# Read lines' norms on GpSimd beside the scans, and one addition for keys and values in the preparation

## The chip, the cores and the metric

The program runs on one core of one Trainium2 chip. The metric is the device time of one execution in microseconds (us), as the median of three runs. The engines are TensorE (PE, with its weight loads as PEld), VectorE (DVE), ScalarE (ACT), GpSimd (POOL) and SyncE (SP); they run side by side and wait for each other by semaphores.

## The reference, cut to what matters

Four layers work on x of 2 x 1024 tokens by 128: an attention (16 heads of 64), a mixture of experts, a second attention (16 heads of 8) whose keys and values are gated, and the experts again. The change lies in what comes ahead of the second attention:

```python
def exterior(p1, p2):                       # 6 products of pairs, per token and head
    L = p1[..., _PI] * p2[..., _PJ] - p1[..., _PJ] * p2[..., _PI]
    n = jnp.clip(jnp.linalg.norm(L, axis=-1, keepdims=True), 1e-12)
    return L / n
write_lines, read_lines = exterior(w1, w2), exterior(r1, r2)
incidence = jnp.einsum('bthp,bshp->bhts', read_lines, write_lines @ J6)
mem_score = jnp.einsum('bhts,hts->bht', incidence ** 2, weights)   # weights: decay ** (t - s), s < t
gram_gate = jax.nn.sigmoid(mem_score * mem_scale[None, :, None])[..., None]
k_enh = k + kv_gate * gram_gate * k_geo
v_enh = v + kv_gate * gram_gate * v_geo
```

## The kernel before

The stages follow each other, each a `Phase` with a block per engine and a barrier at its end. Two of them are touched.

**`geometry` (L1370 to L1757)** makes the gates. Tokens lie on the 128 partitions, eight tiles to each of two batches. ACT copies the projected factors out of PSUM (`moved`, L1523), DVE makes the six components of write and read lines (`cross`, L1633) into `L`. Squared incidence is a sum over 21 products of components. `write_products(b)` (L1649 to L1656) first makes the norms of the write lines from squares that ACT made (`square_write`, L1538), then 21 products; `read_products(b)` (L1672) makes the 15 mixed products of the read lines, while their six squares come from ACT (`square_read`, L1546 and L1547) and stand in the same tile `prod[1]`. The last of the seven instructions of `read_products` waits for them (`read_ready`) and raises `made`, so that PE may transpose. The read lines are not divided by their norm there: `read_scale(b)` (L1638 to L1643, L1681) sums the six squares to `inv`, clips, inverts and multiplies by `mem_scale`, and `weigh(b)` (L1704) applies that to the scores at the end.

PE transposes the products into six PSUM banks (L1491), DVE scans over the tokens (`scan`, L1690) and multiplies (L1698), six scans in all, PE sums (L1460) and turns the scores (L1469), ACT moves them and takes the exponential (L1559, L1553), DVE makes the gates (L1712 to L1714). ACT meanwhile takes sixteen banks of queries in two parts (`queries`, L1530 and L1532), with `square_write(1)` ahead of bank 9 and `square_read(1)` ahead of bank 11; behind the last bank it loads the table of the exponential and makes `dec_e` from the decay (L1584), for which DVE waits before it makes `row_decay` (L1744, L1745) and starts the scans. GpSimd adds the two parts of the queries (L1416), sixteen additions of 128x512, and starts on them when DVE has cleared the first column of the scans (`zeroed`, L1747).

The order on DVE is written out by hand:

```python
            cross(1, slice(0, 2))
            read_scale(0)
            write_products(1)
            read_products(1)
            read_scale(1)
            dve.wait_ge(dec_exp, 1)
```

then the scans of batch 0, two of batch 1, `weigh(0)`, the last scan, `gates(0)`, `weigh(1)`, `gates(1)`.

**`prepare_b` (L1760 to L1847)** makes keys and values of sixteen tiles, in rings of three buffers. PE projects a tile to 512 columns (L1800); DVE multiplies the geometric half by the gate (L1834, `geo`); GpSimd adds the bias (L1847) and, ahead of that, clears the rest of the values' rows (L1844); DVE adds the keys (L1823, `key`) and the values (L1824, into `V9`); ACT makes the rounded copies of the keys (L1812, `rep`); DVE makes their rest (`low`, L1829); PE transposes (L1791) and ACT moves the result to `KS4` (L1815). In its turn i DVE does `geo` of tile i, the additions of tile i-1 and `low` of tile i-2; PE does the projection of tile i and the transposes of tile i-3.

Of the kernel before, what the change touches and what calls it, by code (L numbers as in the profile page):

```python
# [13 lines left out]
P = 128  # L14
# [1352 lines left out]
def geometry(nc, X, stats, xn, xnT, w_geo, sel, decay_logits, scale_row, kv_gate, gate, ident, constants, w_q, q_bias, q_scale, QS4):  # L1367
# [4 lines left out]
    with Phase(nc, "geo") as ph:  # L1372
# [18 lines left out]
        read_ready = ph.sem("read_ready")  # L1391
        turned, used = ph.sem("turned"), ph.sem("used")
        scored, s_moved, flipped = ph.sem("scored"), ph.sem("s_moved"), ph.sem("flipped")
# [14 lines left out]
        @block.gpsimd  # L1408
        def _(pool):
            constants()  # L1410
            pool.wait_ge(zeroed, len(M))
            for k in range(QK):
                g, t = k // 4, k % 4
                dst = QS4[:, g, t * BANK:(t + 1) * BANK]
                pool.wait_ge(q_ready, 2 * k + 2)
                nc.gpsimd.tensor_tensor(dst, dst.bitcast(F32), q_rest[:, g, t * BANK:(t + 1) * BANK], ALU.add)  # L1416
# [174 lines left out]
        def _(dve):  # L1591
# [42 lines left out]

            def norms(b, w, sq):

                n2, part = inv[:, b, w, :, :], T2[:, w * QT:(w + 1) * QT, 0:3, :]
                link(nc.vector.tensor_tensor(part.rearrange("p n c h -> p n (c h)"), sq[:, :, 0:3, :].rearrange("p n c h -> p n (c h)"),  # L1638
                                             sq[:, :, 3:6, :].rearrange("p n c h -> p n (c h)"), ALU.add))
                link(nc.vector.tensor_tensor(n2, part[:, :, 0, :], part[:, :, 1, :], ALU.add))  # L1640
                link(nc.vector.tensor_tensor(n2, n2, part[:, :, 2, :], ALU.add))
                link(nc.vector.tensor_scalar(n2, n2, 1e-24, None, ALU.max))
                link(nc.vector.reciprocal(n2, n2))  # L1643

            def write_products(b):

                line, scaled, out = L[:, b, 0:QT, :, :], T2[:, 0:QT, :, :], prod[0][:, b * QT:(b + 1) * QT, :, :]
                dve.wait_ge(squared, b + 1)
                norms(b, 0, T1[:, 0:QT, :, :])  # L1649
                link(nc.vector.tensor_tensor(scaled, line, inv[:, b, 0, :, :].unsqueeze(2).to_broadcast([P, QT, 6, H]), ALU.mult))  # L1650
# [25 lines left out]

            def read_scale(b):

                dve.wait_ge(lines, 2 * BATCH)
                norms(b, 1, prod[1][:, b * QT:(b + 1) * QT, 0:6, :])  # L1680
                link(nc.vector.tensor_tensor(inv[:, b, 1, :, :], inv[:, b, 1, :, :], scale_row[:, :].unsqueeze(1).to_broadcast([P, QT, H]),  # L1681
                                             ALU.mult))

            def scan(b, g):
# [11 lines left out]
                for c in range(2):  # L1696
                    dve.wait_ge(turned, n + c + 3)
                    nc.vector.scalar_tensor_tensor(RM[j % 3][:, c * BANK:(c + 1) * BANK], bank[(n + 2 + c) % NB][0:ROWS, :],  # L1698
                                                   row_decay[0:ROWS, 0:1], m[:, c * BANK:(c + 1) * BANK], ALU.mult, ALU.mult).then_inc(used, 1)

            def weigh(b):
# [36 lines left out]
            cross(1, slice(0, 2))  # L1738
            read_scale(0)
            write_products(1)  # L1740
            read_products(1)
            read_scale(1)
            dve.wait_ge(dec_exp, 1)
# [7 lines left out]
            scan(1, 0)  # L1751
            scan(1, 1)
            weigh(0)
            scan(1, 2)
            gates(0)
            weigh(1)
# [3 lines left out]
def prepare_b(nc, xnT, w_kv, kv_bias, gate, KS4, V9, ident):  # L1760
# [4 lines left out]
    with Phase(nc, "prep_b") as ph:  # L1765
        geo = [ph.sb(f"geo{i}", [P, 2, H, B_DH]) for i in range(NB)]
        key = [ph.sb(f"key{i}", [P, H, B_DH]) for i in range(NB)]
        rep = [ph.sb(f"rep{i}", [P, NG, GRP, REP, B_DH]) for i in range(NB)]
        kv_ps = [ph.psum(f"kvp{i}", [P, 4, H, B_DH]) for i in range(NB)]
        k_ps = [ph.psum(f"kp{i}", [P, BANK]) for i in range(NB)]  # L1770
        kv_done, gated, biased = ph.sem("kv_done"), ph.sem("gated"), ph.sem("biased")
        keyed, kv_read = ph.sem("keyed"), ph.sem("kv_read")
        high_done, rep_done = ph.sem("high_done"), ph.sem("rep_done")
# [6 lines left out]
        def key_copies(i):  # L1780
            return key[i % NB][:, :, :].unsqueeze(2).to_broadcast([P, H, REP // 2, B_DH])

        @block.tensor
        def _(pe):
# [10 lines left out]
            for i in range(TILES + 3):  # L1795
                if i < TILES:
                    at, b = 1 + (i % QT) * P, i // QT
                    if i >= NB:
                        pe.wait_ge(kv_read, i - NB + 1)
                    nc.tensor.matmul(kv_ps[i % NB][:, :, :, :].rearrange("p w h d -> p (w h d)"), xnT[:, b, at:at + P], w_kv[:, :],  # L1800
# [5 lines left out]
        def _(act):  # L1806
            for i in range(TILES + 2):
                if i < TILES:
                    act.wait_ge(keyed, i + 1)
                    if i >= NB:  # L1810
                        act.wait_ge(k_done, i - NB + 1)
                    nc.scalar.activation(copies(i, 0).bitcast(F32R), key_copies(i), ACT.Copy).then_inc(high_done, 1)  # L1812
                if i >= 2:
                    act.wait_ge(k_done, i - 1)
# [4 lines left out]
        def _(dve):  # L1819
            def add_geo(i):  # L1820

                dve.wait_ge(biased, i + 1)
                nc.vector.tensor_tensor(key[i % NB][:, :, :], kv_ps[i % NB][:, 0, :, :], geo[i % NB][:, 0, :, :], ALU.add).then_inc(keyed, 1)  # L1823
                nc.vector.tensor_tensor(V9[:, i, :, 0:B_DH], kv_ps[i % NB][:, 1, :, :], geo[i % NB][:, 1, :, :], ALU.add).then_inc(kv_read, 1)  # L1824

# [282 lines left out]
```

## Time and profile before

| | |
|---|---|
| median of 3 runs | 1117.47 us (1116.43 to 1118.13) |
| the profiled execution, its own time | 1119.37 us |
| its span, first to last instruction | 1117.6 us, granted TensorE clock 0.924 of full |
| busy | PE 968.8 us (87%), DVE 763.7 (68%), ACT 593.1 (53%), POOL 336.3 (30%) |
| `geometry` | 627.4 to 705.2 us of the span |
| `prepare_b` | 705.5 to 734.6 us |
| second attention | from 734.9 us |

Busy time is a sum over stages that are bound by different engines; what an edit is worth is read in its own stage, from the start times of neighbouring instructions on one engine and from what each waits for. Times in the rows further down are microseconds from the start of the span.

### The profile page before, as it was taken

The numbers are of one execution on the slowest core, as the hardware profiler recorded it, in microseconds if no ns is written. First come the engines' busy times: TensorE is split into PE (matmuls) and PEld (weight loads), VectorE is DVE, ScalarE is ACT, GpSimd is POOL, SyncE is SP. The second block draws the span as 40 slices with busy tenths as digits, with TensorE's granted clock in tenths as the row PEclk, the third lists the DMA queues.
The fourth block names the chain that finished last, engine by engine and source line by source line (L and its number), as shares of the span: only waits on it lengthen the run. The fifth ranks groups of instructions, "written<-read, shape, count | busy, mean of one in ns | idle before, by whom it ended". The sixth has DMA issues, their size and how long they took to land. (4 is left out here: it accounts for less than half of the span.)

```text
span 1117.6 us, 18644 instructions
## 1 busy us (share of the span) xinstructions
PE 968.8 (87%) x6218; PEld 625.2 (56%) x6218; DVE 763.7 (68%) x2256; ACT 593.1 (53%) x1165; POOL 336.3 (30%) x422
## 2 busy tenths in 40 slices
PE   6989999999999999999739376789999999996474
PEld 4767667666667667766429333344444444443363
DVE  6767758775767758777513699787888888863423
ACT  4866657666767658666212291324555555564121
POOL 3522122211221113210144207453644343521523
PEclk9999999999999999999859697868999999999577
DMA  6630000000000000000340100000000000000623
GB/s 206 134 94 2 1 1 1 1 1 1 1 1 1 1 1 1 2 1 1 101 147 29 48 1 0 1 1 1 1 2 1 1 2 1 1 1 13 192 58 99
DMA packets 49402, 32.23 MB, mean 29 GB/s; under 512 B 9195, under 2 KB 45980, under 8 KB 49308
## 3 DMA queue, kind: packets, MB, share of 16 engines
q1 hardware_dynamic: 47260, 26.78, 8.5%
q0 software_dynamic: 2048, 4.26, 1.2%
q8 instruction: 50, 0.82, 0.3%
q14 instruction: 44, 0.36, 0.1%
HBM read 21.44 MB, written 11.69 MB: 30 GB/s over the span
## 5 line engine op out<-in xcount | busy, mean ns | idle before, releaser
L561 ACT ACTIVATE attn_a_prob<-attn_a_score,attn_a_m_all 128x128 f32<-128x128 f32 (+7 forms) x256 | 188.7, 740 | 49.9 <-DVE attn_a_m_all L481 45.8
L911 ACT ACTIVATE attn_b_probT<-attn_b_st 128x1024 f32<-128x1024 f32 (+1 forms) x192 | 145.1, 808 | 131.8 <-PE attn_b_st L777 130.5
L477 DVE TENSOR_REDUCE attn_a_m_far<-attn_a_score 128x1 f32<-128x512 f32 (+3 forms) x192 | 105.6, 550 | 71.5 <-PE attn_a_score L389 68.3
L401 PE MATMUL attn_a_slot<-tab,attn_a_prob 128*128 128x128 f32 x1152 | 149.2, 274 | 0.2
L401 PEld LDWEIGHTS attn_a_slot<-tab,attn_a_prob 128*128 128x128 f32 x1152 | 131.8, 141 | 9.8 <-issue 1.6
L413 PE MATMUL attn_a_o<-attn_a_ptsb,Vd 128*64 128x512 f32 x288 | 136.3, 603 | 0.0
L413 PE MATMUL attn_a_o<-attn_a_ptsa,Vd 128*64 128x512 f32 x288 | 136.3, 603 | 0.0
L840 DVE CUSTOM_DVE_ANT_0 attn_b_slot<-attn_b_slot,later 128x128 f32<-128x128 f32 (+3 forms) x256 | 118.7, 522 | 18.7 <-PE attn_b_slot L752 18.4
L570 ACT ACTIVATE attn_a_ptsa<-attn_a_slot 128x512 f32<-128x512 f32 x144 | 85.7, 595 | 85.9 <-PE attn_a_slot L401 85.4
L752 PE MATMUL attn_b_slot<-KS,attn_b_alone 128*128 128x512 f32 (+2 forms) x384 | 125.6, 424 | 2.7 <-POOL attn_b_alone L933 2.2
L481 DVE CUSTOM_DVE_ANT_0 attn_a_score<-attn_a_score,bias_near,attn_a_m_far 128x256 f32<-128x256 f32 (+2 forms) x192 | 107.4, 559 | 6.8
L490 DVE COPY attn_a_ptsb<-attn_a_slot 128x512 f32<-128x512 f32 x144 | 99.1, 688 | 14.7 <-PE attn_a_slot L401 14.5
L614 POOL COPY attn_a_wide<-attn_a_rinv 128x512 f32<-128x512 f32 x32 | 19.6, 614 | 290.9 <-issue 269.1
L752 PEld LDWEIGHTS attn_b_slot<-KS,attn_b_alone 128*128 128x128 f32 x384 | 63.5, 200 | 73.1 <-DVE attn_b_least L845 20.6
L845 DVE TENSOR_REDUCE attn_b_least<-attn_b_slot 128x1 f32<-128x512 f32 x128 | 80.7, 684 | 19.9 <-PE attn_b_slot L752 19.2
L949 POOL TENSOR_SCALAR_AFFINE_SELECT attn_b_probT<-attn_b_probT 128x256 f32<-128x256 f32 x128 | 51.3, 406 | 124.6 <-ACT attn_b_probT L911 123.3
L792 PE MATMUL attn_b_pv<-attn_b_probT,V 128*32 128x512 f32 (+3 forms) x768 | 83.6, 507 | 0.6 <-POOL attn_b_probT L949 0.6
L933 POOL TENSOR_TENSOR attn_b_alone<-QS,tab 128x512 fp32r<-128x512 f32 x64 | 66.3, 1040 | 42.3 <-PE attn_b_slot L752 39.1
L413 PEld LDWEIGHTS attn_a_o<-attn_a_ptsa,Vd 128*64 128x64 f32 x288 | 34.5, 136 | 60.3 <-issue 50.7
L767 PE MATMUL attn_b_st<-QS,KS 32*128 32x512 f32 (+2 forms) x384 | 56.5, 453 | 2.9 <-ACT attn_b_probT L911 2.2
L389 PE MATMUL attn_a_score<-KH,QS_0a 128*128 128x512 f32 (+2 forms) x96 | 38.1, 397 | 15.7 <-ACT attn_a_prob L561 14.0
L561 ACT ACTIVATION_READ_ACCUMULATOR attn_a_prob<-attn_a_score,attn_a_m_all 128x1 f32 x256 | 51.0, 199 | 0.0
(236 smaller groups left out, 1831.1 us busy)
## 6 DMA issues: line engine op xcount, KB each, us to landing
moe_weights_w<-in_L_ffn_w_dram SPq DMA_DIRECT2D x32, 256.0 KB, 3.4
to_experts<-xn SPq DMA_DIRECT2D x2, 1056.0 KB, 11.8
moe_experts_xe<-to_experts SPq DMA_DIRECT2D x16, 132.0 KB, 2.7
bias_by_query_and_key<-bias_by_distance SPq DMA_DIRECT2D x2, 1024.0 KB
bias_near<-bias_by_query_and_key SPq DMA_DIRECT2D x2, 1024.0 KB, 6.3
from_experts<-xn SPq DMA_DIRECT2D x2, 1024.0 KB, 11.7
moe_experts_back<-from_experts SPq DMA_DIRECT2D x8, 256.0 KB, 3.7
X<-in_L_attn_a_x_dram SPq DMA_DIRECT2D x2, 512.0 KB, 4.7
```

The source lines that it names most:

```text
L401: ins = nc.tensor.transpose(dst[:, jj * P:(jj + 1) * P], probs(g)[:, 2 * jj + half, i * P:(i + 1) * P], ident[:, :])
L413: ins = nc.tensor.matmul(o_ps[OWN[half], :], Vd[:, b * QT + i, OWN[half]], pts[half][k % RING][:, :], start=i == 0, stop=i == steps(g) - 1 ...
L477: nc.vector.tensor_reduce(least, score[t % 2][:, at:at + nk - win], AX.X, ALU.min).then_inc(far_done, 1)
L481: nc.vector.tensor_tensor_reduce(out=near, in0=near, in1=bias_near[:, s * HS + j, BANK - win:], scale=1.0, scalar=least, op0=ALU.add, op1= ...
L490: nc.vector.tensor_copy(pts[1][k % RING][:, :], bank[u % SLOTS_S][:, :]).then_inc(moved_b, 1)
L561: nc.scalar.activation(probs(g)[:, j, 0:nk], score[t % 2][:, at:at + nk], ACT.Exp, bias=m_all[:, j:j + 1], scale=-1.0, accum_out=rowsum[g ...
L570: nc.scalar.activation(pts[0][k % RING][:, :], bank[u % SLOTS_S][:, :], ACT.Copy).then_inc(moved_a, 1)
L752: ins = nc.tensor.matmul(s[:, to:to + wide], alone[j % RING][:, a, :], KS4[:, g, at:at + wide], start=True, stop=True)
L792: ins = nc.tensor.matmul(pv[a * 32:a * 32 + VW, lo:], V9[:, b * QT + kt, g * GRP + a, :], probT[n % 2][:, a, lo:], start=kt == 0, stop=end ...
L840: ins = nc.vector.tensor_tensor_reduce(out=s, in0=s, in1=later[:, BANK - w:], scale=1.0, scalar=3e38, op0=ALU.add, op1=ALU.min, accum_out= ...
L845: nc.vector.tensor_reduce(found, s, AX.X, ALU.min).then_inc(slot_free, 1)
L911: nc.scalar.activation(probT[n % 2][:, two, lo:], st[:, two, lo:], ACT.Exp, scale=-1.0).then_inc(exp_done, 1)
```

## The change

In `geometry` the sums of the read lines' squares and their clipping go from DVE to GpSimd, four instructions per batch, after the wait for `zeroed` and ahead of the query additions; the sum of pairs is written over `L`. On DVE `read_scale(b)` keeps the reciprocal and the product with `scale_row`, and stands in the scans: for batch 0 ahead of `weigh(0)`, for batch 1 behind the last scan. `read_products(1)` now comes before `write_products(1)`. In `prepare_b` one DVE addition of 256 columns, keys and values together, goes to a tile `both`; ACT makes the copies from it and moves the values to `V9`.

```diff
@@ geometry, GpSimd
+            def read_scale(b):
+                pool.wait_ge(made, 2 * b + 2)
+                rows = slice(b * QT, (b + 1) * QT)
+                part, n2 = L[:, b, QT:, 0:3, :], inv[:, b, 1, :, :]
+                nc.gpsimd.tensor_tensor(part, prod[1][:, rows, 0:3, :], prod[1][:, rows, 3:6, :], ALU.add).then_inc(summed, 1)
+                pool.wait_ge(summed, 4 * b + 1)
+                nc.gpsimd.tensor_tensor(n2, part[:, :, 0, :], part[:, :, 1, :], ALU.add).then_inc(summed, 1)
+                pool.wait_ge(summed, 4 * b + 2)
+                nc.gpsimd.tensor_tensor(n2, n2, part[:, :, 2, :], ALU.add).then_inc(summed, 1)
+                pool.wait_ge(summed, 4 * b + 3)
+                nc.gpsimd.tensor_scalar(n2, n2, 1e-24, None, ALU.max).then_inc(summed, 1)
+                pool.wait_ge(summed, 4 * b + 4)
             constants()
             pool.wait_ge(zeroed, len(M))
+            read_scale(0)
+            read_scale(1)
             for k in range(QK):
@@ geometry, DVE
             def read_scale(b):
-                dve.wait_ge(lines, 2 * BATCH)
-                norms(b, 1, prod[1][:, b * QT:(b + 1) * QT, 0:6, :])
+                n2 = inv[:, b, 1, :, :]
+                dve.wait_ge(summed, 4 * b + 4)
+                link(nc.vector.reciprocal(n2, n2))
                 link(nc.vector.tensor_tensor(n2, n2, scale_row[:, :].unsqueeze(1).to_broadcast([P, QT, H]), ALU.mult))
...
             cross(1, slice(0, 2))
-            read_scale(0)
+            dve.wait_ge(lines, 2 * BATCH)
+            read_products(1)
             write_products(1)
-            read_products(1)
-            read_scale(1)
             dve.wait_ge(dec_exp, 1)
...
             scan(1, 1)
+            read_scale(0)
             weigh(0)
             scan(1, 2)
+            read_scale(1)
             gates(0)
@@ prepare_b, PE
                     if i >= NB:
-                        pe.wait_ge(kv_read, i - NB + 1)
+                        pe.wait_ge(summed, i - NB + 1)
@@ prepare_b, ACT
-                    act.wait_ge(keyed, i + 1)
+                    act.wait_ge(summed, i + 1)
                     if i >= NB:
                         act.wait_ge(k_done, i - NB + 1)
                     nc.scalar.activation(copies(i, 0).bitcast(F32R), key_copies(i), ACT.Copy).then_inc(high_done, 1)
+                    nc.scalar.activation(V9[:, i, :, 0:B_DH], both[i % NB][:, 1, :, :], ACT.Copy).then_inc(v_moved, 1)
@@ prepare_b, DVE
                 dve.wait_ge(biased, i + 1)
-                nc.vector.tensor_tensor(key[i % NB][:, :, :], kv_ps[i % NB][:, 0, :, :], geo[i % NB][:, 0, :, :], ALU.add).then_inc(keyed, 1)
-                nc.vector.tensor_tensor(V9[:, i, :, 0:B_DH], kv_ps[i % NB][:, 1, :, :], geo[i % NB][:, 1, :, :], ALU.add).then_inc(kv_read, 1)
+                if i >= NB:
+                    dve.wait_ge(v_moved, i - NB + 1)
+                    dve.wait_ge(rep_done, i - NB + 1)
+                nc.vector.tensor_tensor(both[i % NB][:, :, :, :], kv_ps[i % NB][:, 0:2, :, :], geo[i % NB][:, :, :, :], ALU.add).then_inc(summed, 1)
```

Some places of the order follow, with line numbers of the kernel each is from. First GpSimd in `geometry`, from the clearing of `cols` to the query additions (`QS`, `geo_q_rest`). Before:

```order
L2065 MEMSET cols 128x1024 x2
L1416 TENSOR_TENSOR QS<-QS,geo_q_rest 128x512 [waits geo_q_ready,geo_zeroed]
L1416 TENSOR_TENSOR QS<-QS,geo_q_rest 128x512 [waits geo_q_ready] x15
L79 UNCONDITIONAL_BRANCH
L1841 UNCONDITIONAL_BRANCH [waits barrier_Pool_Activation_PE_DVE_SP_gather]
```

and with the change:

```order
L2085 MEMSET cols 128x1024 x2
L1415 TENSOR_TENSOR geo_L<-geo_prod 128x8x48 [waits geo_made,geo_zeroed]
L1417 TENSOR_TENSOR geo_inv<-geo_L 128x128 [waits geo_summed]
L1419 TENSOR_TENSOR geo_inv<-geo_inv,geo_L 128x128 [waits geo_summed]
L1421 ISA
L1421 TENSOR_SCALAR geo_inv<-geo_inv 128x128 [waits geo_summed]
L1415 TENSOR_TENSOR geo_L<-geo_prod 128x8x48 [waits geo_made,geo_summed]
L1417 TENSOR_TENSOR geo_inv<-geo_L 128x128 [waits geo_summed]
L1419 TENSOR_TENSOR geo_inv<-geo_inv,geo_L 128x128 [waits geo_summed]
L1421 TENSOR_SCALAR geo_inv<-geo_inv 128x128 [waits geo_summed]
L1432 TENSOR_TENSOR QS<-QS,geo_q_rest 128x512 [waits geo_q_ready,geo_summed]
L1432 TENSOR_TENSOR QS<-QS,geo_q_rest 128x512 [waits geo_q_ready] x15
```

Eight instructions stand ahead of the first query addition, and with them an `ISA` row that the diff does not name. Before, GpSimd has such a row ahead of the first `AFFINE_SELECT` of the second attention (L949), and with the change it has none there.

Second, DVE from the end of the fifth scan, where `geo_bank` is the transposed products and `geo_z` the weighed scores. Before:

```order
L1704 TENSOR_TENSOR geo_z<-geo_flip,geo_inv 128x128 [waits geo_flipped]
L1690 SCALAR_TENSOR_TENSOR geo_shared<-geo_row_decay,geo_bank 112x512 [waits geo_turned]
L1690 SCALAR_TENSOR_TENSOR geo_shared<-geo_row_decay,geo_shared,geo_bank 112x512 [waits geo_turned,geo_used]
L1698 SCALAR_TENSOR_TENSOR geo_shared<-geo_bank,geo_row_decay,geo_shared 112x512 [waits geo_turned,geo_scored,geo_used]
L1698 SCALAR_TENSOR_TENSOR geo_shared<-geo_bank,geo_row_decay,geo_shared 112x512 [waits geo_turned]
L1712 TENSOR_SCALAR geo_e<-geo_e 128x128 [waits geo_ez]
L1713 RECIPROCAL geo_z<-geo_e 128x128 [waits geo_chain]
L1714 TENSOR_SCALAR gate_b<-geo_z,kv_gate 128x128 [waits geo_chain]
L1704 TENSOR_TENSOR geo_z<-geo_flip,geo_inv 128x128 [waits geo_flipped]
```

and with the change:

```order
L1714 RECIPROCAL geo_inv<-geo_inv 128x128 [waits geo_summed]
L1715 TENSOR_TENSOR geo_inv<-geo_inv,scale_row 128x128 [waits geo_chain]
L1720 TENSOR_TENSOR geo_z<-geo_flip,geo_inv 128x128 [waits geo_flipped,geo_chain]
L1699 SCALAR_TENSOR_TENSOR geo_shared<-geo_row_decay,geo_bank 112x512 [waits geo_turned]
L1699 SCALAR_TENSOR_TENSOR geo_shared<-geo_row_decay,geo_shared,geo_bank 112x512 [waits geo_turned,geo_used]
L1707 SCALAR_TENSOR_TENSOR geo_shared<-geo_bank,geo_row_decay,geo_shared 112x512 [waits geo_turned,geo_scored,geo_used]
L1707 SCALAR_TENSOR_TENSOR geo_shared<-geo_bank,geo_row_decay,geo_shared 112x512 [waits geo_turned]
L1714 RECIPROCAL geo_inv<-geo_inv 128x128 [waits geo_summed]
L1715 TENSOR_TENSOR geo_inv<-geo_inv,scale_row 128x128 [waits geo_chain]
L1728 TENSOR_SCALAR geo_e<-geo_e 128x128 [waits geo_ez,geo_chain]
L1729 RECIPROCAL geo_z<-geo_e 128x128 [waits geo_chain]
L1730 TENSOR_SCALAR gate_b<-geo_z,kv_gate 128x128 [waits geo_chain]
```

The pair of reciprocal and product for batch 0 stands between the fifth and the sixth scan, that for batch 1 behind the sixth.

## Rows read from the trace of the kernel before

**Rows 1.** Busy time by stretch: us, each engine (instructions), TensorE's granted clock, DMA

```profile
713.50:729.10 15.60, 14.69 (x61) 6.88 (x62) 14.69 (x40) 9.02 (x20) 10.82 (x20) 1.00 0.00 1
...
735.00:760.00 25.00, 23.34 (x60) 12.72 (x60) 21.83 (x74) 1.94 (x2) 13.05 (x13) 0.53 0.01 1
```

**Rows 2.** Timeline, DVE, before the scans: start, us, line, operation, count

```profile
660.65 0.56 DVE L1638 TENSOR_TENSOR geo_shared<-geo_prod 128x384 f32<-128x384 f32 x1
...
663.48 0.56 DVE L1638 TENSOR_TENSOR geo_shared<-geo_shared 128x384 f32<-128x384 f32 x1
...
670.18 2.56 DVE L1672 TENSOR_TENSOR geo_prod<-geo_L 128x256 f32<-128x256 f32 x7
672.66 0.55 DVE L1638 TENSOR_TENSOR geo_shared<-geo_prod 128x384 f32<-128x384 f32 x1
...
674.16 0.95 DVE L1643 RECIPROCAL geo_inv<-geo_inv 128x128 f32<-128x128 f32 x1
...
675.48 0.15 DVE L1744 TENSOR_SCALAR geo_dec_e<-geo_dec_e 112x1 f32<-112x1 f32 x1
```

**Rows 3.** Timeline, ACT, the same stretch

```profile
664.46 0.53 ACT L1547 ACTIVATE geo_prod<-geo_L 128x384 f32<-128x384 f32 x1
...
672.99 0.20 ACT L1584 ACTIVATE geo_dec_e<-decay 112x1 f32<-112x1 f32 x1
```

**Rows 4.** Timeline, DVE, the end of the geometry

```profile
695.46 0.28 DVE L1704 TENSOR_TENSOR geo_z<-geo_flip,geo_inv 128x128 f32<-128x128 f32 x1
695.66 1.21 DVE L1690 TENSOR_TENSOR_SCAN geo_shared<-geo_row_decay,geo_bank 112x512 f32<-112x512 f32 x1
...
699.55 0.22 DVE L1712 TENSOR_SCALAR geo_e<-geo_e 128x128 f32<-128x128 f32 x1
...
703.03 0.29 DVE L1704 TENSOR_TENSOR geo_z<-geo_flip,geo_inv 128x128 f32<-128x128 f32 x1 [1.96 <-PE geo_flip L1469]
```

**Rows 5.** Timeline, all engines, one turn of the preparation in full pace

```profile
716.62 0.42 DVE L1834 TENSOR_TENSOR prep_b_geo<-prep_b_kvp,gate_b 128x256 f32<-128x256 f32 x1 [0.18 <-PE prep_b_kvp L1800]
...
716.96 0.28 DVE L1823 TENSOR_TENSOR prep_b_key<-prep_b_kvp,prep_b_geo 128x128 f32<-128x128 f32 x1
...
717.12 0.72 POOL L1847 TENSOR_TENSOR prep_b_geo<-prep_b_geo,kv_bias 128x256 f32<-128x256 f32 x1 [0.61 <-DVE prep_b_geo L1834]
...
717.36 0.78 DVE L1829 TENSOR_TENSOR prep_b_rep<-prep_b_key,prep_b_rep 128x256 f32<-128x256 f32 x1
...
718.19 0.66 PE L1791 MATMUL prep_b_kp<-tab,prep_b_rep 128*128 128x128 f32 x4 [0.18 <-DVE prep_b_rep L1829]
...
718.68 1.02 PE L1800 MATMUL prep_b_kvp<-w_kv,xnT 128*128 128x512 f32 x2
...
719.74 0.42 DVE L1834 TENSOR_TENSOR prep_b_geo<-prep_b_kvp,gate_b 128x256 f32<-128x256 f32 x1 [0.18 <-PE prep_b_kvp L1800]
```

**Rows 6.** Timeline, DVE, the last `low` but one, with GpSimd idle

```profile
732.38 0.41 DVE L1829 TENSOR_TENSOR prep_b_rep<-prep_b_key,prep_b_rep 128x256 f32<-128x256 f32 x1
```

**Rows 7.** Timeline, POOL, the query additions

```profile
676.06 19.67 POOL L1416 TENSOR_TENSOR QS<-QS,geo_q_rest 128x512 fp32r<-128x512 f32 x16 [46.02 <-DVE geo_shared L1747]
```

**Rows 8.** Line L949 on GpSimd and its sequencer: ns min/median/max, first and last start

```profile
L949 POOLq MODIFY_POOL_CONFIG  x2: 11/11/11, 755.0 to 755.1; - x2
```

**Rows 9.** Timeline, POOL, the first instruction of that line

```profile
758.83 0.41 POOL L949 TENSOR_SCALAR_AFFINE_SELECT attn_b_probT<-attn_b_probT 128x256 f32<-128x256 f32 x1 [3.75 <-ACT attn_b_probT L911]
```

**Rows 10.** Line L862 on DVE: ns min/median/max by form

```profile
L862 DVE SCALAR_TENSOR_TENSOR cols<-attn_b_least,cols x8: 190/192/194, 744.4 to 975.1; 128x16 f32<-128x16 f32 x8
L862 DVE SCALAR_TENSOR_TENSOR cols<-attn_b_both,cols x8: 267/352/358, 766.5 to 997.7; 128x16 f32<-128x16 f32 x8
```

**Rows 11.** Timeline, all engines, one of those beside GpSimd

```profile
798.85 0.89 POOL L949 TENSOR_SCALAR_AFFINE_SELECT attn_b_probT<-attn_b_probT 128x256 f32<-128x256 f32 x2 [0.46 <-ACT attn_b_probT L911]
798.95 0.36 DVE L862 SCALAR_TENSOR_TENSOR cols<-attn_b_both,cols 128x16 f32<-128x16 f32 x1
```

**Rows 12.** Timeline, POOL, the second of those two

```profile
799.34 0.41 POOL L949 TENSOR_SCALAR_AFFINE_SELECT attn_b_probT<-attn_b_probT 128x256 f32<-128x256 f32 x1
```

More of the change, by code:

```diff
@@ L1391, in geometry @@
         read_ready = ph.sem("read_ready")
-        turned, used = ph.sem("turned"), ph.sem("used")
+        turned, used, summed = ph.sem("turned"), ph.sem("used"), ph.sem("summed")
         scored, s_moved, flipped = ph.sem("scored"), ph.sem("s_moved"), ph.sem("flipped")
@@ L1633, in cross, with norms @@
                 nc.vector.tensor_tensor(dst, first, second, ALU.subtract).then_inc(lines, halves.stop - halves.start)
-            def norms(b, w, sq):
-                n2, part = inv[:, b, w, :, :], T2[:, w * QT:(w + 1) * QT, 0:3, :]
+            def norms(b, sq):
+                n2, part = inv[:, b, 0, :, :], T2[:, 0:QT, 0:3, :]
                 link(nc.vector.tensor_tensor(part.rearrange("p n c h -> p n (c h)"), sq[:, :, 0:3, :].rearrange("p n c h -> p n (c h)"),
@@ L1648, in write_products @@
                 dve.wait_ge(squared, b + 1)
-                norms(b, 0, T1[:, 0:QT, :, :])
+                norms(b, T1[:, 0:QT, :, :])
                 link(nc.vector.tensor_tensor(scaled, line, inv[:, b, 0, :, :].unsqueeze(2).to_broadcast([P, QT, 6, H]), ALU.mult))
@@ L1675, in read_products @@
                 ins.then_inc(made, 1)
-            def read_scale(b):
-                dve.wait_ge(lines, 2 * BATCH)
-                norms(b, 1, prod[1][:, b * QT:(b + 1) * QT, 0:6, :])
-                link(nc.vector.tensor_tensor(inv[:, b, 1, :, :], inv[:, b, 1, :, :], scale_row[:, :].unsqueeze(1).to_broadcast([P, QT, H]),
-                                             ALU.mult))
             def scan(b, g):
@@ L1699, in scan, with read_scale @@
                                                    row_decay[0:ROWS, 0:1], m[:, c * BANK:(c + 1) * BANK], ALU.mult, ALU.mult).then_inc(used, 1)
+            def read_scale(b):
+                n2 = inv[:, b, 1, :, :]
+                dve.wait_ge(summed, 4 * b + 4)
+                link(nc.vector.reciprocal(n2, n2))
+                link(nc.vector.tensor_tensor(n2, n2, scale_row[:, :].unsqueeze(1).to_broadcast([P, QT, H]), ALU.mult))
             def weigh(b):
@@ L1766, in prepare_b @@
         geo = [ph.sb(f"geo{i}", [P, 2, H, B_DH]) for i in range(NB)]
-        key = [ph.sb(f"key{i}", [P, H, B_DH]) for i in range(NB)]
+        both = [ph.sb(f"both{i}", [P, 2, H, B_DH]) for i in range(NB)]
         rep = [ph.sb(f"rep{i}", [P, NG, GRP, REP, B_DH]) for i in range(NB)]
@@ L1771, in prepare_b @@
         kv_done, gated, biased = ph.sem("kv_done"), ph.sem("gated"), ph.sem("biased")
-        keyed, kv_read = ph.sem("keyed"), ph.sem("kv_read")
+        summed, v_moved = ph.sem("summed"), ph.sem("v_moved")
         high_done, rep_done = ph.sem("high_done"), ph.sem("rep_done")
@@ L1780, in key_copies @@
         def key_copies(i):
-            return key[i % NB][:, :, :].unsqueeze(2).to_broadcast([P, H, REP // 2, B_DH])
+            return both[i % NB][:, 0, :, :].unsqueeze(2).to_broadcast([P, H, REP // 2, B_DH])
         @block.tensor
```

## The prediction

> **What bounds the kernel now.** The chain of waits covers only the end of the span, from 1064.9 us on, and says nothing on the changed stretch; so I read the busy time by stretch first, then the timelines of single engines there. In the preparation's full pace DVE and PE are both busy 14.69 of 15.60 us [rows 1]: a tie, which busy shares can't break. From 660.65 us to the start of the scans DVE goes from instruction to instruction without a wait [rows 2], so it sets the pace there, and through the scans as well; only 1.96 us ahead of the last `weigh` are idle [rows 4].
>
> **Edit 1, in front of the scans: a gain of 2.24 us, not of what leaves DVE.** `read_scale(0)` takes from 660.65 to 663.48, 2.83 us; `read_scale(1)` from 672.66 to 675.48, 2.82 us [rows 2]. So 5.65 us leave this stretch. But the order has changed too. `read_products(1)` lasts 672.66 - 670.18 = 2.48 us, and now starts at 660.65. Its seventh instruction waits for the squares of ACT, which end at 664.46 + 0.53 = 664.99 [rows 3]; before, it came at 672 and waited for nothing. ACT's place for them behind ten banks of queries isn't changed. Without that wait the six first would be through by about 662.9, so DVE stands for 2 us, does the last (0.2) and begins `write_products(1)` at 665.2. That takes 670.18 - 663.48 = 6.70 us [rows 2]: through at 671.9. Then comes the second wait: `dec_e`, the exponential of the decay, which ACT ends at 672.99 + 0.20 = 673.19 [rows 3]. Before, DVE came by at 675.48, long after. Now ACT sets the start of the scans: 673.24 instead of 675.48. **Gain 2.24 us.** ACT's own work there depends on DVE only through `lines`, at 660.6, which doesn't move.
>
> **Edit 2, what comes back inside the scans.** Reciprocal and product are 675.48 - 674.16 = 1.32 us [rows 2]. The pair for batch 0 lies between the fifth and the sixth scan, where DVE has no gap (695.46 to 695.66 is `weigh` alone [rows 4]): it costs its full 1.32 us. The pair for batch 1 lies behind the sixth scan: from there DVE has `gates(0)`, 699.55 to 701.07 by the idle time in the row, then 1.96 us idle until the scores are turned [rows 4]. The pair fills 1.32 of these, 0.64 us are left: nothing. If that cover is gone, each us more costs one.
>
> **Edit 3, two readers of one port.** `low` (L1829) takes 0.78 us in full pace [rows 5] and 0.41 us when GpSimd does nothing [rows 6]. GpSimd's addition beside it runs from 717.12 to 717.84; `low` starts at 717.36 and ends at 718.14, 0.30 us behind that addition, in all turns alike. I read this as `low` standing until GpSimd has read. The same with L862: 0.19 us alone, up to 0.36 beside GpSimd [rows 10]. All of these have two inputs in SBUF; DVE's scans, with one input in PSUM, don't differ beside GpSimd and without it. The product of `inv` and `scale_row` has two inputs in SBUF, and in its new place, about 694.3 us, it meets the query additions, which stand back to back at 19.67 / 16 = 1.23 us each [rows 7]. So it waits between 0 and 1.23 us on the path; nothing in the trace fixes the phase and I take the middle, **0.6 us**. It should get in between two of them: at 798.95 DVE's L862 stood behind the first of two adjacent instructions of GpSimd and ended at 799.31, before the second began at 799.34 [rows 11, 12].
>
> The Trainium skill says the same and draws the line sharply: a DVE instruction with two SBUF inputs and a GpSimd instruction that reads SBUF exclude each other, and the second to issue is blocked for the whole of the first (SBUF — State Buffer, "Who interferes with whom"). By this the trace agrees, with 0.78 against 0.41; the rule speaks against both halves of this change.
>
> **Edit 4, GpSimd's eight instructions.** The addition of 256 columns takes 0.72 us [rows 5], of 512 1.23 us [rows 7]; 384 columns lie between, 1.0, and 128 follow at 0.5. The clipping has one input: not over the 0.41 us of L949's 256 columns [rows 9]. Per batch 1.0 + 0.5 + 0.5 + 0.4 and four semaphores of 0.08 (717.04 to 717.12 [rows 5]) make 2.7 us, 5.4 for both. GpSimd starts 2.24 us earlier, at 673.8, so the query additions begin at 679.2 and end at 698.9. The stage ends at 705.2 (table), now about 704.9: 6 us of cover. The sums are needed at 693.2: no wait.
>
> The `ISA` row is the unknown. Before, it stands in the second attention as MODIFY_POOL_CONFIG at 755.1 [rows 8], and the first instruction behind it starts at 758.83, just when ACT has released it [rows 9]. So such a change of configuration costs between 0 and 758.83 - 755.1 = 3.7 us. Anywhere in that range the query additions end at 698.9 to 702.6, before 704.9, and it costs nothing by itself. Its leaving the second attention gains nothing, as the wait there is for ACT.
>
> The Trainium skill gives about 6 us for the first call after such a load (GPSIMD Engine Reference, "Instruction dispatch"). The trace disagrees for the instruction that it shows, which began 3.7 us behind it. By the page's figure GpSimd would end at 704.9 instead, at the very end of the stage: a result of its own, taken as a rival below.
>
> **Edit 5, the preparation: nothing.** Two additions, together 0.40 us from start to start (716.96 to `low` at 717.36), become one like `geo`, 0.34 us (716.62 to 716.96 [rows 5]): 0.06 us less DVE work per tile, 0.9 us over sixteen. But what follows, `low`, waits for the port until GpSimd's addition is read, and that starts when `geo` ends. The loop is `geo` at 716.62, GpSimd 717.12 to 717.84, `low` to 718.14, transposes from 718.19, projection from 718.68 to 719.70, `geo` at 719.74 [rows 5]: 3.12 us for two tiles, and neither addition is in it. So 0, with 0.9 us as the other end of the range. ACT gets a move of 128 columns more per tile, between its 0.20 us for one column and its 0.53 us for 384 [rows 3], and is busy 9.02 of 15.60 [rows 1], ten tiles: at the most 14.3: covered, and if it weren't, `rep` would come late to `low`. The new waits of DVE, on `v_moved` and `rep_done`, are for three tiles back and are long met; behind them would stand `low`. In the last tile the copies start 0.14 us later, as the joint addition ends later, and ACT ends with at most 0.1 us more.
>
> **The sum**: -2.24 + 1.32 + 0.6 + 0 + 0.05 = -0.3 us. Against the profiled execution's own 1119.37 that is 1119.1; that execution lies 1.90 above the median, so against the median of 1117.47 it is **1117.2 us**. With the ends of each term: -2.24 + 1.32 + 0 - 0.9 = -1.8 to -2.24 + 1.32 + 1.23 + 0.1 = +0.4. 0.2%, or 2.2 us, is about what a measurement can tell from no change here, and all of this lies within it.
>
> **Rivals.**
>
> *The product starves at the port* (slower). GpSimd's query additions queue without a gap. If one takes the port again before DVE gets it, the product stands from 694.3 until they are through, at 698.9 to 702.6 by edit 4: 4.6 to 8.3 us, of which the forecast has 0.6. Time 1121.2 to 1124.9. It decides as soon as DVE loses a second round. For it: sixteen ready additions. Against it: DVE got in at 799.31 [rows 11, 12]. 6%.
>
> *GpSimd gets late* (no change to little slower). With the configuration at 3.7 us or more the query additions are still there when DVE does the product of batch 1 and the steps of `gates(0)`, from 700.2 on; each may wait up to 1.23 us, and only 0.64 us are free ahead of the last `weigh`. Two such waits at 0.6 cost 0.6 us, four full ones over 4. Time 1117.8, at most 1121. GpSimd itself becomes the end only if the eight instructions and the load take over 704.9 - 673.8 - 19.7 = 11.4 us. For it: the price of small additions at strides isn't in the trace. Against: 6 us of cover. 14%, of it 2% beyond 2.2 us.
>
> *The preparation was bound by DVE's total, and the clock moves* (faster). If `low` didn't wait for GpSimd's read, all 0.9 us would come. And PE runs at the lower level, 1.2 GHz, through nearly all of the first 25 us of the second attention (0.53 of full at 735 to 760 [rows 1]), after it stood still at the seam between the stages. DVE's work in there is 21.83 us, so at the full clock it could be up to 25 - 21.83 = 3.2 us shorter. A shift of the start can change which stretches are slow, though nothing in the change shortens the pause. Time 1117.2 - 0.9 - 3.2 = 1113.1. 10%, and 2% for the opposite, a stretch that falls to the lower level.
>
> **How the numbers follow.** The forecast has 68%, 1117.2, its own range 1115.6 to 1118.4 with the scatter of the runs. The late GpSimd (14%) and small gains of the preparation without the clock stay within 0.2% too. Faster by over 0.2%: the clock, 10%. Slower: starvation 6%, a very late GpSimd 2%, the clock 2%, 10% in all. Same: 80%. The range leaves out the clock's gain and the starvation: 1115.0 to 1119.3.
>
> **What would show it.** In the profile after: the seventh instruction of `read_products(1)` starts at about 665.0; `dec_e + 1` starts within 0.1 us of ACT's exponential; the scans start 2.2 us earlier; the first product L1715 lasts 0.3 to 1.5 us, the last scan starts about 0.3 us earlier than before; the query additions end before 703; `low` still lasts about 0.78 and ends 0.3 us behind GpSimd's addition; two tiles still take 3.12 us. I am wrong if the two-tile pace falls to 3.06 or less (then DVE's total counts), if L1715 lasts over 1.6 us (starvation), or if GpSimd starts the query additions later than 685.

## The result: slower by 3.8 us

Over nine runs each, the kernel before took 1118.78 us in the median (1116.43 to 1120.18) and the changed one 1122.63 us (1120.1 to 1123.64). The ratio is 1.0034, with a 95% interval of 1.0025 to 1.0042: 3.8 us slower, 2.8 to 4.7. The forecast was no change, 1117.2, with a range up to 1119.3; the time lies above it. The kernel before itself came out 1.31 us higher over nine runs than over the three that the forecast started from (1118.78 against 1117.47), so the fair comparison is by differences: -0.3 us forecast, +3.8 measured.

### The profile after

Its span is 1120.6 us against 1117.6, at a granted clock of 0.922. Everything in front of the changed code stands about 1.05 us later in this execution (the third `cross` ends at 661.67 against 660.62), which is taken as scatter between executions, since nothing ahead of it was changed, and is taken off wherever stretches are compared.

The timeline of DVE, in front of the scans (columns: start, duration, engine, line, operation, count, and in brackets the idle time before it with what ended it):

```profile
661.70 2.37 DVE L1688 TENSOR_TENSOR geo_prod<-geo_L 128x256 f32<-128x256 f32 x6
666.07 0.29 DVE L1688 TENSOR_TENSOR geo_prod<-geo_L 128x128 f32<-128x128 f32 x1 [2.00 <-ACT geo_prod L1563]
...
674.27 0.15 DVE L1759 TENSOR_SCALAR geo_dec_e<-geo_dec_e 112x1 f32<-112x1 f32 x1 [1.22 <-ACT geo_dec_e L1600]
```

ACT at the same place:

```profile
665.51 0.53 ACT L1563 ACTIVATE geo_prod<-geo_L 128x384 f32<-128x384 f32 x1
...
672.75 1.28 ACT L1600 ACT_TABLE_LOAD   x1
674.04 0.20 ACT L1600 ACTIVATE geo_dec_e<-decay 112x1 f32<-112x1 f32 x1
```

Both waits of edit 1 are there: 2.00 us for ACT's squares, 1.22 us for the exponential of the decay. The scans' first step is at 674.27 instead of 675.48 + 1.05 = 676.53: 2.26 us earlier. That much is gained.

GpSimd, its new instructions and the query additions; then the view of line L1421 with the duration as ns min/median/max; then the same view of the query additions:

```profile
674.86 0.99 POOL L1415 TENSOR_TENSOR geo_L<-geo_prod 128x384 f32<-128x384 f32 x1 [44.13 <-DVE geo_shared L1762]
...
680.41 19.65 POOL L1432 TENSOR_TENSOR QS<-QS,geo_q_rest 128x512 fp32r<-128x512 f32 x16
```

```profile
L1421 POOLq MODIFY_POOL_CONFIG  x2: 7/7/7, 676.9 to 676.9; - x2
L1421 POOL TENSOR_SCALAR geo_inv<-geo_inv x2: 524/532/539, 677.0 to 679.8; 128x128 f32<-128x128 f32 x2
```

```profile
L1432 POOL TENSOR_TENSOR QS<-QS,geo_q_rest x16: 1262/1274/1289, 680.4 to 698.8; 128x512 fp32r<-128x512 f32 x16
```

The eight instructions take 680.41 - 674.86 = 5.55 us, and behind the change of configuration at 676.9 the instruction starts at 677.0: no wait to speak of. The additions end at 700.06. Each lasts 1.27 us, but one starts every 1.23 us: they overlap by 0.04.

DVE and GpSimd around the first product, from the timeline of all engines (a window that begins in it counts only four of the additions), and the end of the stage on DVE:

```profile
694.26 0.94 DVE L1714 RECIPROCAL geo_inv<-geo_inv 128x128 f32<-128x128 f32 x1
...
695.13 4.92 POOL L1432 TENSOR_TENSOR QS<-QS,geo_q_rest 128x512 fp32r<-128x512 f32 x4
695.24 4.96 DVE L1715 TENSOR_TENSOR geo_inv<-geo_inv,scale_row 128x128 f32<-128x128 f32 x1
700.24 0.29 DVE L1720 TENSOR_TENSOR geo_z<-geo_flip,geo_inv 128x128 f32<-128x128 f32 x1
```

```profile
705.31 0.29 DVE L1715 TENSOR_TENSOR geo_inv<-geo_inv,scale_row 128x128 f32<-128x128 f32 x1
...
707.81 0.29 DVE L1720 TENSOR_TENSOR geo_z<-geo_flip,geo_inv 128x128 f32<-128x128 f32 x1 [0.64 <-PE geo_flip L1485]
...
712.40 0.42 DVE L1854 TENSOR_TENSOR prep_b_geo<-prep_b_kvp,gate_b 128x256 f32<-128x256 f32 x1 [2.39 <-PE prep_b_kvp L1817]
```

Here the time went. The product, 0.29 us of work when it stands alone (705.31), lasted 4.96 us, from 0.11 us behind the start of an addition to 0.14 us behind the end of the last one, past four additions. The row shows no idle time: to the profile a stalled instruction is a busy one. The rest is as forecast: the second pair costs nothing, and 0.64 us stay free ahead of the last `weigh`.

One turn of the preparation, DVE, GpSimd and ACT:

```profile
718.27 0.42 DVE L1854 TENSOR_TENSOR prep_b_geo<-prep_b_kvp,gate_b 128x256 f32<-128x256 f32 x1 [0.18 <-PE prep_b_kvp L1817]
...
718.61 0.41 DVE L1844 TENSOR_TENSOR prep_b_both<-prep_b_kvp,prep_b_geo 128x256 f32<-128x256 f32 x1
...
718.77 0.72 POOL L1867 TENSOR_TENSOR prep_b_geo<-prep_b_geo,kv_bias 128x256 f32<-128x256 f32 x1 [0.61 <-DVE prep_b_geo L1854]
718.94 0.84 DVE L1849 TENSOR_TENSOR prep_b_rep<-prep_b_both,prep_b_rep 128x256 f32<-128x256 f32 x1
...
719.38 0.29 ACT L1830 ACTIVATE V<-prep_b_both 128x128 f32<-128x128 f32 x1
...
719.44 0.41 POOL L1864 MEMSET V<- 128x384 f32 x1
...
721.39 0.42 DVE L1854 TENSOR_TENSOR prep_b_geo<-prep_b_kvp,gate_b 128x256 f32<-128x256 f32 x1 [0.18 <-PE prep_b_kvp L1817]
```

721.39 - 718.27 = 3.12 us for two tiles, as in [rows 5]. `low` starts 0.17 us behind the start of GpSimd's addition instead of 0.24, and lasts 0.84 us instead of 0.78; it still ends 0.29 us behind that addition. It got in although GpSimd's next instruction, the `memset` at 719.44, starts 0.05 us before the addition's recorded end; the `memset` has no input, so it reads nothing. Busy time, in the columns of [rows 1], of the same 15.60 us of the preparation and of the first 25 us of the second attention:

```profile
718.30:733.90 15.60, 14.72 (x61) 6.87 (x61) 14.72 (x31) 11.12 (x31) 10.84 (x20) 1.00 0.00 1
739.80:764.80 25.00, 23.24 (x60) 12.74 (x60) 21.82 (x74) 1.94 (x2) 13.06 (x13) 0.53 0.00 1
```

DVE is as busy as before, 14.72 of 15.60, though it has nine instructions less there (31 against 40): what they freed is stall in `low`. The granted clock is 0.53 behind the seam in both kernels, and the second attention takes as long in both (its last mask on GpSimd, L949, starts at 1023.8 against 1019.1, 4.7 us later, where the attention itself starts 4.8 us later), so the clock has no part in the difference.

The account: -2.26 in front of the scans, +4.67 for the standing (4.96 - 0.29), +1.31 for reciprocal and product inside the scans (700.24 - 694.26 = 5.98, less the 4.67), 0 in the preparation: +3.72. The first step of the preparation is indeed 712.40 - 707.62 - 1.05 = 3.73 us later, and the medians differ by 3.85. The two profiled spans differ by 3.0 only, 1.05 of it in front: behind the second attention this one execution was some 1.7 us shorter, in stages that the change doesn't touch. The rows give the account and the medians its size; the two spans alone would give neither.

### The profile page after: what moved, and what is told of

It reads as the page before. It is cut to its first block and busy times, and to the rows that moved or that the text cites. A ratio compares the mean times of both kernels' runs of the same rounds, so it can differ in the third digit from the quotient of the medians.

```text
span 1120.6 us, 18660 instructions
## 1 busy us (share of the span) xinstructions
PE 967.7 (86%) x6218; PEld 624.9 (56%) x6218; DVE 764.9 (68%) x2232; ACT 596.2 (53%) x1181; POOL 340.7 (30%) x430
## 5 line engine op out<-in xcount | busy, mean ns | idle before, releaser
L949 POOL TENSOR_SCALAR_AFFINE_SELECT attn_b_probT<-attn_b_probT 128x256 f32<-128x256 f32 x128 | 51.3, 407 | 124.4 <-ACT attn_b_probT L911 123.2
L933 POOL TENSOR_TENSOR attn_b_alone<-QS,tab 128x512 fp32r<-128x512 f32 x64 | 66.3, 1040 | 42.3 <-PE attn_b_slot L752 39.2
```

## The experiments

All ratios are against the kernel before, run on the same chip at the same time. Theory: the product waits at a port that GpSimd's additions, overlapping by 0.04 us, never let go. Rivals: something else in the geometry, or the preparation.

**Each half alone.** The first kernel has the change in `geometry` only, the second that in `prepare_b` only.

> The change in the geometry alone, the preparation as before. Theory (the product of inv and scale_row is kept from GpSimd's read port until the query additions are through): all of the loss is here, the product lasts about 5.0 us as in the changed kernel, time 3.7 us above the kernel before. Rival (the joint addition in the preparation costs something too): under 3 us above.

> The change in the preparation alone, the geometry as before. Theory (low waits for GpSimd's addition, neither DVE addition is in the loop): two tiles still take 3.12 us, time as before within 0.3 us. Rival (DVE's total sets the pace): two tiles in 3.0, 0.9 us faster.

The geometry alone: 1119.49 us against 1114.71, ratio 1.0045 (1.0029 to 1.0062). The preparation alone: 1114.99, ratio 1.0003 (0.9993 to 1.0013). The loss is all in the geometry: there the preparation's first step lies 38.14 us behind `dec_e + 1` (709.91 - 671.77), against 32.14 before and 38.13 in the changed kernel. `low` and the pace in the second are those of the changed kernel. The timeline of DVE with the geometry alone:

```profile
692.74 4.98 DVE L1715 TENSOR_TENSOR geo_inv<-geo_inv,scale_row 128x128 f32<-128x128 f32 x1
```

**One gap in the additions.** GpSimd waits ahead of its fourteenth addition until DVE has done `weigh(0)`, which stands behind the product:

```diff
                 pool.wait_ge(q_ready, 2 * k + 2)
+                if k == 13:
+                    pool.wait_ge(nz, 1)
```

> The changed kernel, but GpSimd waits ahead of query addition 13 until weigh(0) is done. Theory (DVE gets the port only when GpSimd has nothing ready that reads): the product lasts for the rest of addition 12 and its own 0.3 us, about 1.5 us, and the time falls by 3.5 us from the changed kernel, to 0.2 us above the kernel before. Rival (the product is slow because it shares the port and crawls through all of its 128 columns): it still lasts over 2.5 us, and what is gained is what GpSimd's pause gives.

The timeline of DVE, and that of GpSimd:

```profile
692.82 1.31 DVE L1717 TENSOR_TENSOR geo_inv<-geo_inv,scale_row 128x128 f32<-128x128 f32 x1
```

```profile
677.97 16.00 POOL L1434 TENSOR_TENSOR QS<-QS,geo_q_rest 128x512 fp32r<-128x512 f32 x13
694.60 3.70 POOL L1434 TENSOR_TENSOR QS<-QS,geo_q_rest 128x512 fp32r<-128x512 f32 x3 [0.62 <-DVE geo_z L1722]
```

1114.94 us, ratio 1.0001 (0.9991 to 1.001): the whole loss is gone with one wait on another engine. The product ends 0.16 us behind the thirteenth addition (677.97 + 16.00 = 693.97), so it gets in at the first break, and doesn't crawl beside GpSimd for a time of its own.

**The product one scan earlier.** `read_scale(0)` stands ahead of `scan(1, 1)`, so more additions are still to come:

> The changed kernel, with reciprocal and product of batch 0 ahead of the fifth scan instead of behind it, 3.9 us earlier. Theory (it stands until the last query addition is through): the product lasts 5.0 + 3.9 = 8.9 us and ends at the same time as in the changed kernel, about 25.3 us behind the start of the first scan; the whole time is that of the changed kernel. Rival (a fixed cost of some 5 us for this instruction beside GpSimd, or a limited number of lost rounds, four): it lasts 5.0 us again, and ends 3.9 us earlier.

The timeline of DVE, and that of GpSimd in a window that begins with the product:

```profile
687.80 8.88 DVE L1715 TENSOR_TENSOR geo_inv<-geo_inv,scale_row 128x128 f32<-128x128 f32 x1
```

```profile
686.70 9.83 POOL L1432 TENSOR_TENSOR QS<-QS,geo_q_rest 128x512 fp32r<-128x512 f32 x8
```

It lasted 8.88 us, until 0.15 us behind the end of the last addition (696.53). Its end goes with GpSimd's queue and not with its own place: it isn't the instruction that is dear.

The other half of that expectation, the time of the changed kernel, fails in the rows: the product ends at the same place, but now the fifth scan still stands behind it, and the preparation's first step lies 42.04 us behind `dec_e + 1` (712.76 - 670.72) instead of 38.13, another 3.91 us lost. The one run's 1117.76 us hides this. In its second attention the granted clock was 0.84 in the third 10 us against 0.62 in the changed kernel (1.2 GHz would be 0.50), and from the attention's first step on DVE to its last mask 279.0 us passed instead of 282.5. Why the clock rose earlier in this execution stays open.

**How wide must a break be?** The additions are made to wait for each other:

```diff
-                nc.gpsimd.tensor_tensor(dst, dst.bitcast(F32), q_rest[...], ALU.add)
+                nc.gpsimd.tensor_tensor(dst, dst.bitcast(F32), q_rest[...], ALU.add).then_inc(summed, 1)
+                pool.wait_ge(summed, 8 + k + 1)
```

> The changed kernel, but each query addition raises a semaphore and GpSimd waits for it before the next, so that 0.08 us lie between two. Theory (DVE gets the port in any gap in which GpSimd holds nothing; 0.08 us between two semaphored instructions is one): the product waits for one addition at most, 0.3 to 1.6 us, and the time falls to between 1 us below and 0.6 above the kernel before. Rival (a gap must be longer than that, as GpSimd's next instruction is already waiting for the port): the product still stands to the last addition, by then 16 times 0.1 us later, and the time is 1 to 2 us above the changed kernel.

1118.03 us against 1119.25, ratio 0.9987 (0.9977 to 0.9997), and the additions take 21.64 us instead of 19.65: one starts every 1.35 us instead of 1.23, 0.12 more. Both products lasted 0.29 us. But each came just at a seam between two additions (the first at 696.92; the addition that starts at 696.94 lasted 1.39 us, so there GpSimd gave way), and this said nothing on a product that already stands. Two more kernels shifted the phase, the first with four small fills by GpSimd, the second with an idle reciprocal of 128x64 on DVE ahead of the product:

> Kernel: that with the query additions one by one (each waits for the one before, which leaves about 0.08 us between two), with four small fills by GpSimd in front of them, so that the additions stand some tenths of a microsecond later and the product of batch 0 no longer comes just at a gap. Theory (any gap on GpSimd is enough for DVE to get the port): the product starts within an addition and lasts until that addition is through, 0.4 to 1.6 us, and the next addition starts late by its 0.3 us. Rival (a gap of 0.08 us is too short, and the two products of 0.29 us of that kernel were chance): it lasts until the last addition, some 5 us or more.

> Kernel: that with the query additions one by one, and DVE makes one further reciprocal of 128x64 numbers (about 0.5 us, its result is not used) between the reciprocal and the product of batch 0. The shift by the fills of GpSimd was only 0.2 us and the product still fell on a seam between two additions; this one puts it about 0.5 us into an addition. Theory (the break between two additions that wait for each other is enough): the product starts about 0.5 us behind an addition's start and lasts until a little after that addition's end, 0.7 to 1.2 us, and the next addition starts 0.1 to 0.3 us late. Rival (the break is too short for a product that already stands): it lasts until the last addition, some 5 us.

Each was run once, 1120.05 us beside 1119.27 and 1113.71 beside 1113.67, so only their rows are read. The fills moved the additions by 0.2 us only; the product began 0.12 us before an addition's recorded end (696.71, 696.83) and again lasted 0.29 us: a miss. The reciprocal put it into an addition. Timeline of all engines there, and of GpSimd from within that addition:

```profile
691.67 0.55 DVE L1718 RECIPROCAL geo_q_pause<-geo_inv 128x64 f32<-128x64 f32 x1
692.26 0.82 DVE L1719 TENSOR_TENSOR geo_inv<-geo_inv,scale_row 128x128 f32<-128x128 f32 x1
693.11 0.29 DVE L1724 TENSOR_TENSOR geo_z<-geo_flip,geo_inv 128x128 f32<-128x128 f32 x1
```

```profile
691.66 2.60 POOL L1433 TENSOR_TENSOR QS<-QS,geo_q_rest 128x512 fp32r<-128x512 f32 x2
...
693.00 1.26 POOL L1433 TENSOR_TENSOR QS<-QS,geo_q_rest 128x512 fp32r<-128x512 f32 x1
```

The addition began at 691.66 and lasts 1.27: until 692.93. The product began at 692.26, stood for 0.53 us, and ended at 693.08, 0.15 us behind it; the next addition, at 693.00, wasn't late. So among these additions a recorded break of 693.00 - 692.93 = 0.07 us is enough for a DVE instruction that stands, and an overlap of 0.04 us isn't. It is one case. A wait as such isn't what lets DVE in: the additions of the changed kernel wait too, each for a `q_ready` that was raised long before, and have no break.

The overlap alone isn't what shuts DVE out. `low` got in ahead of a `memset` that overlaps the addition by 0.05 us (above), and the kernel before has a case ahead of an instruction that reads. The timeline of all engines there:

```profile
766.25 0.43 POOL L949 TENSOR_SCALAR_AFFINE_SELECT attn_b_probT<-attn_b_probT 128x256 f32<-128x256 f32 x1
766.46 0.27 DVE L862 SCALAR_TENSOR_TENSOR cols<-attn_b_both,cols 128x16 f32<-128x16 f32 x1
...
766.65 1.03 POOL L933 TENSOR_TENSOR attn_b_alone<-QS,tab 128x512 fp32r<-128x512 f32 x1
```

L862, 0.19 us alone [rows 10], ended at 766.73, 0.05 us behind the `affine_select` (766.68), though L933 is recorded from 766.65 on. What closes the seam between two query additions, and leaves this one open, no run here shows.

**The product without its port.** GpSimd multiplies by the reciprocal of `mem_scale`, and DVE keeps the reciprocal alone:

> The changed kernel, with the product taken from DVE: GpSimd multiplies the sums by the inverse of mem_scale (made once by DVE, early), DVE keeps the reciprocal, which has one input. Theory: in front of the scans -2.24, in the scans +0.99 for the reciprocal, nothing stands; 1.25 us below the kernel before. Rival (the reciprocal also stands beside GpSimd): no gain, or a loss.

1118.28 us, ratio 0.9994 (0.9984 to 1.0004). The forecast gain of 1.25 lies in the interval, but so does none. The rows agree with it: from `dec_e + 1` to the preparation's first step 33.13 us pass (707.84 - 674.71) against 32.14 before, +0.99 as forecast, with the 1.22 us of wait for ACT in front as in the changed kernel. The product's standing is gone; another instruction stands one place further, as the additions now end at 701.59 (681.92 + 19.67). The timeline of DVE:

```profile
700.75 0.93 DVE L1730 TENSOR_SCALAR geo_e<-geo_e 128x128 f32<-128x128 f32 x1
...
703.92 0.23 DVE L1730 TENSOR_SCALAR geo_e<-geo_e 128x128 f32<-128x128 f32 x1 [0.38 <-ACT geo_e L1572]
```

The first of these has one input, in SBUF, and lasted until 0.09 us behind the last addition. It cost nothing here, as 0.26 us stay free ahead of the last `weigh`. So two inputs aren't needed to be stopped by GpSimd; beside the same additions the reciprocal (0.94 us) and `weigh`, with one input in PSUM (0.29 us), weren't stopped.

**The preparation's real bound.** In the kernel before, `low(i - 2)` is put ahead of `add_geo(i - 1)`, where GpSimd's addition is not yet released:

> The kernel before, with low(i-2) ahead of the two additions of tile i-1 in DVE's turn; no instruction more or less. Theory (low stands for GpSimd's addition and is in the loop that sets the pace): low now comes before that addition has begun, lasts 0.41 us, the loop is 2.4 us for two tiles and PE's own 1.43 us per tile sets the pace, 2.86 instead of 3.12: 8 x 0.26 = 2 us below the kernel before. Rival (low is slow by its form or by ACT beside it): it still lasts 0.78, no gain.

The timeline of all engines:

```profile
716.76 0.42 DVE L1829 TENSOR_TENSOR prep_b_rep<-prep_b_key,prep_b_rep 128x256 f32<-128x256 f32 x1
716.93 0.84 POOL L1847 TENSOR_TENSOR prep_b_geo<-prep_b_geo,kv_bias 128x256 f32<-128x256 f32 x1
...
717.72 0.42 DVE L1834 TENSOR_TENSOR prep_b_geo<-prep_b_kvp,gate_b 128x256 f32<-128x256 f32 x1
...
719.02 0.42 DVE L1834 TENSOR_TENSOR prep_b_geo<-prep_b_kvp,gate_b 128x256 f32<-128x256 f32 x1
```

1115.97 us against 1119.25, ratio 0.997 (0.996 to 0.9981). Now `low` holds the port first and GpSimd waits, 0.84 instead of 0.72 us, where nobody waits for it. A tile takes 1.30 us instead of 1.56, and the stage 26.0 us instead of 29.1. That is more than the 2 us expected: TensorE's 1.43 us a tile, taken as the next bound, wasn't one. Edit 5 made one of DVE's two additions and won nothing; turning the order of the same instructions won 3.1 us. Two things went out of the way of `low` together, its standing (0.37 us) and the two additions ahead of it (0.40 us), and this run doesn't tell their shares apart.

**All together.** The whole change, the multiplication on GpSimd, `low` first, and the things that edit 1 had left waiting: ACT makes the decay's exponential ahead of the queries and both squares of batch 1 at the ninth bank, and both `read_scale` stand behind the last scan:

> The changed kernel with the scale on GpSimd, low ahead of the joint addition, the exponential of the decay ahead of the queries on ACT, both squares at bank 9, both reciprocals behind the last scan. Theory: the scans start 5.4 us earlier than in the kernel before (no wait for ACT's squares nor for its exponential), nothing stands in them, up to 0.8 us come back behind them, the preparation gives 2: about 7 us below the kernel before. Rival (PE's transposes, which wait for ACT's later queries, then hold the scans, or the tensor_scalar of the gates stands beside the query additions): the scans stretch by 1 us or more, 4 to 6 us below.

1113.09 us against 1119.25, ratio 0.9937 (0.992 to 0.9955): 6.2 us less, 5.0 to 9.0, which holds both the theory's 7 and part of the rival's 4 to 6. The timeline of DVE:

```profile
672.66 0.15 DVE L1761 TENSOR_SCALAR geo_dec_e<-geo_dec_e 112x1 f32<-112x1 f32 x1
...
698.70 0.92 DVE L1729 TENSOR_SCALAR geo_e<-geo_e 128x128 f32<-128x128 f32 x1
```

No wait is left in front of the scans: from the end of the third `cross` to `dec_e + 1` it is 9.42 us (663.24 to 672.66) against 14.86, 5.4 less as expected. `gates(0)` still stood 0.69 us, until just behind the last addition. The preparation takes 26.9 us, not the 26.0 of `low` first alone, though a tile takes 1.30 us in both: with `low` first the joint addition costs 0.9 us at the stage's start and end, where the last two `low` wait 0.48 us for ACT's copies instead of 0.28. So this version beats both kernels, and without edit 5 it may be better still; that combination wasn't run.

## Why the prediction was wrong

- **Edit 1 was right**, size and cause: 2.26 us against 2.24, and both waits on ACT where they were placed.
- **Edit 2 was right**: the first pair cost 1.31 us against 1.32, the second nothing, with 0.64 us left over.
- **Edit 3 is the step that failed.** That the product meets the additions at the port was right. But "It should get in between two of them" took 0.6 us where it was 4.67. It argued from [rows 11, 12], where DVE's instruction had got in ahead of GpSimd's second. There the second starts 0.49 us behind the first, which lasts 0.41: a break of 0.08 us. The query additions have none, and the kernel before held this already. Its line view of them:

```profile
L1416 POOL TENSOR_TENSOR QS<-QS,geo_q_rest x16: 1259/1282/1293, 676.1 to 694.4; 128x512 fp32r<-128x512 f32 x16
```

One starts every 1.23 us [rows 7] and lasts 1.28. "Back to back" was taken for the same thing in both places. The run with the product inside an addition confirms the row for what it shows: with 0.07 us of break DVE does get in. The forecast's own sign for this, L1715 over 1.6 us, came true; its other two signs didn't (3.12 us for two tiles, query additions from 680.41, well ahead of 685).
- The Trainium skill's rule (SBUF — State Buffer, "Who interferes with whom") has the second to issue blocked for the whole of the first instruction. Read as one instruction it gives at most 1.23 us, and the trace disagrees, with 4.96 and 8.88 us: what has to end here is the unbroken row of additions.
- **Edit 4 was right**: 5.55 us for eight instructions against 5.4, and the change of configuration at the bottom of its range, under 0.1 us. The Trainium skill's 6 us for a first call (GPSIMD Engine Reference, "Instruction dispatch") isn't what this load cost.
- **Edit 5 was right**: nothing, and for the reason given as far as the rows show it, as `low` starts earlier and still ends 0.29 us behind GpSimd's addition. The run with `low` first shows that the place of `low` set the pace; how much of that is the port it doesn't separate.
- **The rivals.** The product starving at the port, at 6%, is what happened: additions through at 699.01 with the 1.05 us taken off, in its range of 698.9 to 702.6, and 4.67 us of standing at the lower end of its 4.6 to 8.3. The condition on which it was to decide ("as soon as DVE loses a second round") was right, and it should have had the larger chance, since the one row against it showed a row of instructions with breaks. The late GpSimd and the clock had no part in the result. But that the clock can shorten the second attention by up to 3.2 us, as its rival had it, is borne out by the single run above with 3.5 us.

With a pause on GpSimd the kernel came to 1.0001 of the one before, and with additions that wait for each other to 0.9987: about the forecast for the change without the standing. Without edit 3's error the rest of the sum holds.

## What to carry to other kernels

Work that moves to GpSimd or DVE is priced by who holds the shared port meanwhile: look in the new place for a long row of like GpSimd instructions that have nothing left to wait for, and compare their pace with their single duration. Where the pace was the shorter, as with these sixteen additions, a DVE instruction with two SBUF inputs stood until the whole row was through, in each of the three kernels that put one beside the whole row. A semaphore wait behind each addition (0.12 us for each), or one wait at the right place, cut that to the rest of one addition. Where a DVE instruction always ends the same 0.3 us behind one of GpSimd, try their order before removing work.

## What was not expected of the hardware

- A DVE product of 0.29 us lasted 4.96 and 8.88 us beside unbroken GpSimd additions, and stood 0.53 us only where the breaks are 0.07 us.
- A tensor_scalar of 128x128 float32 with a single SBUF input is stopped too: 0.92, 0.93 and, with additions one by one, 1.17 and 1.19 us, instead of 0.23.
- Behind a change of GpSimd's configuration the instruction started within 0.1 us.
- Whoever comes first holds the port: `low` first costs GpSimd 0.12 us, GpSimd first costs `low` 0.37 to 0.43 us.
